# An adaLN block with attention and experts: experts three batches behind in 512-column products, queries and keys two ahead, bias added by GpSimd

## The chip, the cores and the metric

The kernel runs on one core of a Trainium2 chip. The metric is the device time of one execution in microseconds (us). Engines are named as the profile names them: PE is TensorE (PEld its weight loads), DVE VectorE, ACT ScalarE, POOL GpSimd, SP the engine that only issues DMAs.

## What is computed

16 batches of 256 tokens of 128 channels, in float32:

```python
mod = (silu(c) @ wmod).reshape(16, 6, 1, 128)            # sa, ca, ga, sb, cb, gb per batch
ga, gb = sign(ga) * max(|ga|, 0.25), the same for gb
h = layernorm(x) * (1 + ca) + sa
q, k, v = split(h @ Wqkv + bqkv)                         # 16 heads of 8 channels
Kmat = exp(-r_sigma * (|k_i|^2 + |q_j|^2 - 2 k_i . q_j))
x = x + ga * ((Kmat @ v) @ Wproj + bproj)
h = layernorm(x) * (1 + cb) + sb
mask = top 2 of softmax(h @ w_router.T + b_router)       # of 8 experts, weight 1 each
x = x + gb * sum_e mask_e * (h @ w_experts[e].T + b_experts[e])
```

## The kernel before, in words

The work is a software pipeline written out by hand: each engine has a function `step(k)` which lists its instructions for step k in order, with semaphore waits. Steps -2 and -1 are the prologue, 0 to 14 are pipelined, then come `last` (step 15) and `tail`. Step k does the attention of batch k and the other stages of batches around it. Each engine works strictly in the order of its list.

Per batch: GpSimd makes the first layernorm (`rsqrt`, `normalise`, into xn), TensorE transposes it (`turn_x`), ScalarE scales and shifts it (h1), TensorE multiplies it by the weights of queries and keys (`qk_rows`, L1001) and of the values (`values`, L1010). DVE adds the bias to queries and keys twice, into qkf and, rounded to fp32r, into hl (`queries_keys`, `high_parts`); GpSimd makes squares (sq, L411) and the low part (hl, L413); TensorE sums the squares (`norms`, L1023), ScalarE and DVE split the result (norm_hi, norm_parts, L731). SP stacks high parts, low parts and norms by DMA (`stack`) into st, of which there are two, by the parity of the batch. With that stacking one product per head gives the whole exponent.

Four score groups a step (`qk_scores(k, g)`, L962) each fill the four banks of `scores`; ScalarE takes the exponentials in two halves (L495); `pv` (L982) multiplies them by the values, in 32-column strips of the array. ScalarE copies the result out (o_sb), `project` (L1048) multiplies by wg, which GpSimd has made (`weigh`, L394, and L396, which adds the projection's bias to x); DVE adds to x (`first_residual`, L746), takes statistics (L688), GpSimd the root, DVE normalises (`normalise`, x2n), TensorE transposes (`turn_x2`, L1056), ScalarE scales (h2), DVE splits h2 in a high and a low fp32r part (`split_h2`), TensorE multiplies by the router weights (`router`, L1064). DVE's `choose` makes the mask of the two best experts: logits (L776), top 8, their indices, eq (L787), mask (L790).

The experts are four groups c of two experts each (`experts(b, c)`, L1120 to L1122). A group has, for each half of the tokens, three products of 256 columns: high by high, low by high, high by low. DVE multiplies each expert's 128 columns by its mask column and accumulates in acc (L708), 16 instructions a batch. The accumulator starts from the experts' bias: the mask is transposed (`turn_mask`), multiplied by the biases (`expert_bias`, L1084) and copied by ScalarE into acc. GpSimd's `gate` multiplies acc by the gate (L382) and adds it to x (L385).

What is done in step k before: queries and keys, norms and values of batch k+1; pv of k-1 (second half of group 2, and 3) and of k (groups 0, 1, half of 2); projection of k-1; router, mask and groups 0 and 1 of the experts of k-2, groups 2 and 3 of k-3; gate of k-3.

The ways in which products use the array matter here. Scores and the bias product have 32 or 16 rows; queries and keys, values, norms, pv, projection and router have 32 columns and lie side by side in strips; the experts' products and the transposes of xn and x2n take the full array.

## Time and profile before

| | |
|---|---|
| median of 3 runs | 221.42 us (221.41 to 222.49) |
| profiled execution | 223.4 us, of which the span from first to last instruction 221.6 |
| mean granted TensorE clock | 0.992 |
| steady step (from 60.6 us to 184.5 us of the span) | 12.06 us |
| first scores, step 0 | 14.66 us |
| first scores of step 1, 2, 3 and 15 | 25.43, 36.61, 48.57, 193.23 us |

The profile is of one execution. Busy time counts the time in which at least one instruction runs on an engine; the ends of products are modelled. In a timeline each row is a run of like instructions: its start, the time from its start to the end of the last, engine, line, operation, operands, number; idle time of the engine ahead of it stands in brackets with what released it. A product appears twice as often in it as in the program where its operands are float32 and not fp32r.

### The profile page before, as it was taken

The page shows a single profiled execution, that of the slowest core. Times are in us where ns is not written, and L with a number is a line of the kernel's source. Part 1 is how long each engine was busy: PE and PEld are TensorE (multiplying, and loading weights), DVE is VectorE, ACT ScalarE, POOL GpSimd, SP SyncE. Part 2 cuts the span into 40 slices and gives each one's busy share as a digit, 9 for nine tenths or more (in the row PEclk, how much of TensorE's full clock was granted, in tenths as well). Part 3 has the DMA queues.
Part 4 walks back from the last instruction along what each step waited for, and adds up shares of the span by engine and source line. Part 5 has one row for each costly group of instructions (what it writes and reads, how often), then busy time and mean ns, then how long its engine had stood idle before and what let it go on. Part 6 is the DMA issues. An engine that isn't in the chain of part 4 may idle for free.

```text
span 221.6 us, 8225 instructions
## 1 busy us (share of the span) xinstructions
PE 211.3 (95%) x3250; PEld 148.2 (67%) x3250; DVE 176.4 (80%) x610; ACT 163.5 (74%) x234; POOL 138.3 (62%) x204
## 2 busy tenths in 40 slices
PE   7979889899999999999999999999999999999993
PEld 6656454567676767677677767676767767666791
DVE  5876442768888898988898888889898889877884
ACT  5236888877877868698877788686879777787362
POOL 5455756564957758575849486675857594434183
PEclk9996999999999999999999999999999999999999
DMA  5565233332323332434333332324341423200001
GB/s 152 150 209 180 71 114 104 114 105 104 114 74 127 106 119 86 151 89 148 96 144 74 104 129 81 125 81 143 86 151 68 149 67 120 79 24 27 3 24 49
DMA packets 22472, 22.94 MB, mean 104 GB/s; under 512 B 2330, under 2 KB 20258, under 8 KB 22434
## 3 DMA queue, kind: packets, MB, share of 16 engines
q1 hardware_dynamic: 21962, 21.79, 30.3%
q10 hardware_dynamic: 472, 0.62, 0.9%
q8 instruction: 26, 0.43, 0.8%
q14 instruction: 12, 0.10, 0.2%
HBM read 6.65 MB, written 2.12 MB: 40 GB/s over the span
## 4 chain that ended last, share of the span: by engine, by line
PE 88%; ACT 3%; issue 2%; DVE 2%; POOL 2%; DMA 1%; POOLq 0%; DVEq 0%; ACTq 0%
PE att_ps L982 26%; PE scores L962 12%; PE qkv_ps L1001 7%; PE qkv_ps L1010 4%; PE qkv_ps L1120 3%; PE mid_ps L1048 3%; PE ffn_ps L1120 3%; PE ffn_ps L1122 3%; PE ffn_ps L1121 3%; ACT probs L495 3%; PE att_ps L1120 2%; PE scores L914 2%; PE mid_ps L1084 2%; PE qkv_ps L1122 2%; PE qkv_ps L1121 2%
## 5 line engine op out<-in xcount | busy, mean ns | idle before, releaser
L495 ACT ACTIVATE probs<-scores 128x1024 f32<-128x1024 f32 x128 | 124.3, 1022 | 12.1 <-PE scores L962 7.1
L982 PE MATMUL att_ps<-probs,vpad 128*32 128x256 f32 x1024 | 68.0, 382 | 0.0
L982 PEld LDWEIGHTS att_ps<-probs,vpad 128*32 128x32 f32 x1024 | 29.6, 109 | 17.7 <-issue 0.2
L962 PE MATMUL scores<-st 32*128 32x256 f32 x512 | 37.3, 329 | 4.2 <-ACT probs L495 2.7
L368 POOL TENSOR_TENSOR ve<-stats,eps 128x2 f32<-128x2 f32 x32 | 6.3, 195 | 44.8 <-DVE stats L688 44.8
L708 DVE SCALAR_TENSOR_TENSOR acc<-ffn_ps,mask,acc 128x128 f32<-128x128 f32 x114 | 32.0, 343 | 0.2
L962 PEld LDWEIGHTS scores<-st 32*128 32x128 f32 x512 | 23.1, 183 | 13.2 <-ACT probs L495 4.7
L411 POOL TENSOR_TENSOR sq<-qkf 128x512 f32<-128x512 f32 x15 | 15.6, 1042 | 20.8 <-DVE qkf L714 20.8
L375 POOL TENSOR_SCALAR xn<-x_all,stats,rstd 128x128 f32<-128x128 f32 x30 | 25.8, 863 | 1.6
L370 POOL TENSOR_TENSOR rstd<-ve,expo 128x2 f32<-128x2 f32 x32 | 22.8, 711 | 2.5
L708 DVE SCALAR_TENSOR_TENSOR acc<-qkv_ps,mask,acc 128x128 f32<-128x128 f32 x64 | 18.0, 344 | 7.3 <-PE qkv_ps L1122 7.3
L714 DVE TENSOR_TENSOR qkf<-qkv_ps,bqk_col 128x512 f32<-128x512 f32 x16 | 11.1, 692 | 12.1 <-PE qkv_ps L1001 12.0
L413 POOL TENSOR_TENSOR hl<-qkf,hl 128x512 fp32r<-128x512 f32 x15 | 19.4, 1292 | 0.0
L1001 PE MATMUL qkv_ps<-h,wqk_sb 128*32 128x256 f32 x256 | 17.1, 385 | 0.0
L1120 PE MATMUL ffn_ps<-we_hi,h_hi 128*128 128x256 f32 x56 | 17.1, 305 | 0.0
L502 ACT COPY acc<-mid_ps 128x256 f32<-128x256 f32 x15 | 5.6, 372 | 14.8 <-PE mid_ps L1084 14.8
L1121 PE MATMUL ffn_ps<-we_hi,h_lo 128*128 128x256 f32 x56 | 15.6, 279 | 0.0
L1122 PE MATMUL ffn_ps<-we_lo,h_hi 128*128 128x256 f32 x56 | 15.6, 279 | 0.0
L708 DVE SCALAR_TENSOR_TENSOR acc<-att_ps,mask,acc 128x128 f32<-128x128 f32 x52 | 14.6, 343 | 0.2 <-DVE acc L708 0.2
L382 POOL TENSOR_TENSOR gated<-acc,rb_all 128x256 f32<-128x256 f32 x14 | 10.3, 737 | 5.2 <-DVE acc L708 4.5
L688 DVE BATCH_NORM_STATS2 stats<-x_all 128x6 f32<-128x256 f32 x32 | 12.5, 423 | 0.1
L396 POOL TENSOR_TENSOR x_all<-x_all,rb_all 128x256 f32<-128x256 f32 x16 | 11.8, 739 | 0.0
(172 smaller groups left out, 429.6 us busy)
## 6 DMA issues: line engine op xcount, KB each, us to landing
st<-hl SPq DMA_DIRECT2D x47, 256.0 KB
rb_all<-rb_rows SPq DMA_DIRECT2D x16, 192.0 KB, 3.2
out_dram<-x_all SPq DMA_DIRECT2D x16, 128.0 KB, 1.8
x_all<-in_L_attn_x_dram SPq DMA_DIRECT2D x13, 128.0 KB, 3.0
st<-norm_parts SPq DMA_DIRECT2D x60, 16.0 KB
we_sb<-in_L_ffn_w_experts_dram SPq DMA_DIRECT2D x1, 512.0 KB, 5.4
w_mod_sb<-in_L_wmod_dram SPq DMA_DIRECT2D x1, 256.0 KB, 4.6
st<-hl ACTq DMA_DIRECT2D x1, 256.0 KB
```

The costliest lines, as they stand in the source:

```text
L370: nc.gpsimd.tensor_tensor(rstd[:, n, :], ve[:, n, :], expo[:, :], ALU.pow).then_inc(rstd_ok, 1)
L375: i = nc.gpsimd.tensor_scalar(xn[:, par, t * C:(t + 1) * C], x_all[:, b, t * C:(t + 1) * C], stats[:, 0, par, 3 * t + 1:3 * t + 2], rstd[: ...
L411: nc.gpsimd.tensor_tensor(sq[:, :, :], qkf[:, :, :], qkf[:, :, :], ALU.mult).then_inc(sq_ok, 1)
L413: nc.gpsimd.tensor_tensor(hl[:, 1:4:2, :], qkf[:, :, :], hl_f[:, 0:4:2, :], ALU.subtract).then_inc(lo_ok, 1)
L495: nc.scalar.activation(probs[:, g, 2 * half:2 * half + 2, :], scores[:, 2 * half:2 * half + 2, :], ACT.Exp, scale=two_sigma).then_inc((exp ...
L708: v.scalar_tensor_tensor(acc[:, q, t, :], y, m, acc[:, q, t, :], ALU.mult, ALU.add).then_inc(acc_step, 1)
L962: i = pe.matmul(scores[:, r, t * T:(t + 1) * T], st[rows, par, g, t * P:(t + 1) * P], st[rows, par, g, T:2 * T], start=True, stop=True)
L982: i = pe.matmul(att_ps[r * ROWS:(r + 1) * ROWS, 0:T], heads[:, g * ROWS:(g + 1) * ROWS], probs[:, g, r, t * T:(t + 1) * T], start=(g == 0 ...
L1001: i = pe.matmul(qkv_ps[m, a * T:(a + 1) * T], wqk_sb[:, a, m], h1[:, :], start=True, stop=True)
L1120: pe.matmul(dst, hi, we_hi[:, es], start=True, stop=False)
L1121: pe.matmul(dst, lo, we_hi[:, es], start=False, stop=False)
L1122: i = pe.matmul(dst, hi, we_lo[:, es], start=False, stop=True)
```

## The change

- The experts of batches 0 to 12 (`b < WIDE`, WIDE = NB - 3) are made three steps behind. A group c is now half c // 2 of the experts for half c % 2 of the tokens: three products of 512 columns. Batches 13 to 15 keep 256 columns.
- acc has two accumulators per batch for them; the first instruction into each is a multiplication, and nothing is loaded beforehand. The bias product goes, a step later, through ScalarE into bias_sb, and GpSimd's `gate`, now four steps behind, first adds the two accumulators, then bias_sb.
- Queries and keys (with high parts and low parts) are made two steps ahead, norms and values one ahead; h1 has two buffers. The first layernorm runs three ahead on GpSimd.
- The order of each engine's list is new; pv of a batch is in whole groups. The warm-up products of step 0 are gone. SP stacks a batch only when the scores of the one two before it are done.

The diff, cut to what is spoken of:

```diff
+    HE = NE // 2
+    WIDE = NB - 3
...
-        h1 = sb("h1", [P, T])
+        h1 = sb("h1", [P, 2, T])
...
-        acc = sb("acc", [P, 2, NT, C])
+        acc = sb("acc", [P, 2, 2, NT, C])
+        bias_sb = sb("bias_sb", [P, NT * C])
...
@@ stack (SP)
+                else:
+
+                    sp.wait_ge(qk_a, G * (b - 1))
+                    sp.wait_ge(qk_b, G * (b - 1))
...
@@ gate (GpSimd)
+                if b < WIDE:
+                    nc.gpsimd.tensor_tensor(wide, acc[:, par, 0, :, :], acc[:, par, 1, :, :], ALU.add).then_inc(both_ok, 1)
+                    pool.wait_ge(both_ok, b + 1)
+                    pool.wait_ge(bias_in, b + 1)
+                    nc.gpsimd.tensor_tensor(gated[:, par, :], gated[:, par, :], bias_sb[:, :], ALU.add).then_inc(bias_out, 1)
+                    pool.wait_ge(bias_out, b + 1)
...
@@ step (GpSimd), k > 0
+                if has(k - 4):
+                    gate(k - 4)
+                if has(k + 2):
+                    parts(k + 2)
+                if k > 0:
+                    weigh(k)
                 if has(k - 1):
                     rsqrt(1, k - 1, (k + 1) % 2, bn2, ve2, rstd2)
+                if k > 0 and has(k + 3):
+                    first_norm(k + 3)
...
@@ experts (VectorE)
+                if b < WIDE:
+
+                    h, t = c // NT, c % NT
+                    if c == 0 and b >= 2:
+                        dve.wait_ge(both_ok, b - 1)
+                    for e in range(HE):
+                        j = HE * c + e
+                        y = bank[:, e * C:(e + 1) * C]
+                        m = mask[:, q, t, 0, HE * h + e:HE * h + e + 1].bitcast(F32)
+                        a = acc[:, q, e % 2, t, :]
+                        if h == 0 and e < 2:
+                            v.tensor_scalar(a, y, m, None, ALU.mult).then_inc(acc_step, 1)
+                        else:
+                            dve.wait_ge(acc_step, STEPS * b + j - 1)
+                            v.scalar_tensor_tensor(a, y, m, a, ALU.mult, ALU.add).then_inc(acc_step, 1)
+                    return
...
@@ experts (TensorE)
+                if b < NB - 4 and c == 0:
+                    pe.wait_ge(norm_ok, b + 5)
+                elif b < NB - 4 and c == 1:
                     pe.wait_ge(o_ok, b + 3)
+                elif b < NB - 4 and c == 2:
+                    pe.wait_ge(m_sb, b + 1)
+                elif b < NB - 4:
+                    pe.wait_ge(acc_step, steps(b, 3 * HE))
...
-                for t in range(NT):
-                    dst = f_bank(b, c)[:, t * EC * C:(t + 1) * EC * C]
+
+                for t in (c % NT,) if b < WIDE else range(NT):
+                    dst = f_bank(b, c) if b < WIDE else f_bank(b, c)[:, t * EC * C:(t + 1) * EC * C]
...
@@ step (TensorE)
                 qk_scores(k, 0)
+                if has(k - 4):
+                    expert_bias(k - 4)
...
+                if k > 1:
+                    norms(k + 1)
                 if has(k - 1):
-                    pv(k - 1, 2, (1,))
-                if has(k - 1):
+                    pv(k - 1, 2)
                     pv(k - 1, 3)
...
+                if has(k - 3):
+                    turn_mask(k - 3)
+                qk_scores(k, 1)
...
+                if has(k - 3):
+                    experts(k - 3, 0)
+                    experts(k - 3, 1)
+                if has(k - 2):
+                    turn_x2(k - 2)
+                if k > 0 and has(k + 2):
+                    turn_x(k + 2)
+                if has(k - 3):
+                    experts(k - 3, 2)
+                qk_scores(k, 2)
...
+                if k > 0 and has(k + 2):
+                    qk_rows(k + 2)
+                pv(k, 0)
+                values(k + 1)
...
                 if has(k - 2):
                     router(k - 2)
+                qk_scores(k, 3)
+                if has(k - 1):
+                    project(k - 1)
+                pv(k, 1)
...
+                if has(k - 3):
+                    experts(k - 3, 3)
```

Three places show how the lists move. A row is a line, an operation, its output and inputs (buffer numbers left out), its shape and how many stand in a row.

On PE, in a steady step of before, from the half group of pv to the second of two expert groups that lie around the transposes (the last three rows come once more right behind):

```order
L982 MATMUL att_ps<-probs,vpad 32x256 x4
L1120 MATMUL qkv_ps<-we_hi,h_hi 128x256
L1121 MATMUL qkv_ps<-we_hi,h_lo 128x256
L1122 MATMUL qkv_ps<-we_lo,h_hi 128x256
L1120 MATMUL qkv_ps<-we_hi,h_hi 128x256
L1121 MATMUL qkv_ps<-we_hi,h_lo 128x256
L1122 MATMUL qkv_ps<-we_lo,h_hi 128x256
L1056 MATMUL mid_ps<-ident,x2n 128x128 x2
L1035 MATMUL mid_ps<-ident,xn 128x128 x2
L1120 MATMUL ffn_ps<-we_hi,h_hi 128x256
L1121 MATMUL ffn_ps<-we_hi,h_lo 128x256
L1122 MATMUL ffn_ps<-we_lo,h_hi 128x256
```

Now, from score group 1 on:

```order
L1056 MATMUL scores<-st 128x256 x8
L1253 MATMUL qkv_ps<-we_hi,h_hi 128x512
L1254 MATMUL qkv_ps<-we_hi,h_lo 128x512
L1255 MATMUL qkv_ps<-we_lo,h_hi 128x512
L1253 MATMUL att_ps<-we_hi,h_hi 128x512
L1254 MATMUL att_ps<-we_hi,h_lo 128x512
L1255 MATMUL att_ps<-we_lo,h_hi 128x512
L1165 MATMUL mid_ps<-ident,x2n 128x128 x2
L1138 MATMUL mid_ps<-ident,xn 128x128 x2
L1253 MATMUL ffn_ps<-we_hi,h_hi 128x512
L1254 MATMUL ffn_ps<-we_hi,h_lo 128x512
L1255 MATMUL ffn_ps<-we_lo,h_hi 128x512
```

Three of the four groups stand in one stretch around the transposes, with half as many products of twice the columns, and score groups on both sides of it.

On DVE, from the mask of one batch on, before (hl here and below is one tensor's name, written by two engines):

```order
L787 TENSOR_TENSOR eq<-slot_e,topi 128x32
L790 TENSOR_TENSOR mask<-eq 128x32
L708 SCALAR_TENSOR_TENSOR acc<-att_ps,mask,acc 128x128 x4
L746 TENSOR_TENSOR x_all<-mid_ps,x_all 128x256
L731 SCALAR_TENSOR_TENSOR norm_parts<-norm_hi,lo_col,qkv_ps 128x128
L688 BN_STATS stats<-x_all 128x6 x2
L762 CAST mask_t<-mid_ps 16x256
L756 TENSOR_SCALAR x2n<-x_all,stats,rstd 128x128 x2
L767 CAST h_hi<-h 128x256
L769 TENSOR_TENSOR h_lo<-h,h_hi 128x256
L738 TENSOR_TENSOR vpad<-qkv_ps,bq_all 128x32x8
L708 SCALAR_TENSOR_TENSOR acc<-ffn_ps,mask,acc 128x128 x4
```

Now:

```order
L873 TENSOR_TENSOR eq<-slot_e,topi 128x32
L876 TENSOR_TENSOR mask<-eq 128x32
L825 TENSOR_TENSOR x_all<-mid_ps,x_all 128x256
L748 BN_STATS stats<-x_all 128x6
L817 TENSOR_TENSOR vpad<-mid_ps,bq_all 128x32x8
L748 BN_STATS stats<-x_all 128x6
L768 SCALAR_TENSOR_TENSOR acc<-ffn_ps,mask,acc 128x128 x4
L851 CAST h_hi<-h 128x256
L853 TENSOR_TENSOR h_lo<-h,h_hi 128x256
L835 TENSOR_SCALAR x2n<-x_all,stats,rstd 128x128 x2
L810 SCALAR_TENSOR_TENSOR norm_parts<-norm_hi,lo_col,qkv_ps 128x128
```

The expert group moved from behind mask to behind the statistics, split_h2 (h_hi, h_lo) now stands ahead of normalise (x2n), and norm_parts, for which PE's first expert group waits, comes after all of them.

On POOL, from the first layernorm to the low parts of queries and keys, before:

```order
L375 TENSOR_SCALAR xn<-x_all,stats,rstd 128x128 x2
L382 TENSOR_TENSOR gated<-acc,rb_all 128x256
L385 TENSOR_TENSOR x_all<-x_all,gated 128x256
L394 TENSOR_TENSOR wg<-wproj_sb,rb_all 128x128
L396 TENSOR_TENSOR x_all<-x_all,rb_all 128x256
L411 TENSOR_TENSOR sq<-qkf 128x512
L413 TENSOR_TENSOR hl<-qkf,hl 128x2x256
```

Now, and on to weigh:

```order
L399 TENSOR_SCALAR xn<-x_all,stats,rstd 128x128 x2
L408 TENSOR_TENSOR gated<-acc 128x256
L411 TENSOR_TENSOR gated<-gated,bias_sb 128x256
L413 TENSOR_TENSOR gated<-gated,rb_all 128x256
L416 TENSOR_TENSOR x_all<-x_all,gated 128x256
L435 TENSOR_TENSOR sq<-qkf 128x512
L437 TENSOR_TENSOR hl<-qkf,hl 128x2x256
L425 TENSOR_TENSOR wg<-wproj_sb,rb_all 128x128
L427 TENSOR_TENSOR x_all<-x_all,rb_all 128x256
```

gate has two additions more and comes ahead of sq and hl, and weigh (wg and the addition to x) moved from ahead of sq to right behind hl.

## Rows read from the trace of the kernel before

**Rows 1.** The page, part 1: busy time by engine.

```profile
PE 211.3 (95%) x3250; PEld 148.2 (67%) x3250; DVE 176.4 (80%) x610; ACT 163.5 (74%) x234; POOL 138.3 (62%) x204
```

**Rows 2.** By stage: us; busy of PE, PEld, DVE, ACT, POOL; clock, DMA share, GB/s.

```profile
14.66:25.43 10.77, 9.87 (x124) 6.05 (x125) 6.24 (x10) 7.24 (x9) 6.36 (x7) 0.84 0.35 115
25.43:36.61 11.18, 9.48 (x157) 5.30 (x158) 3.69 (x9) 9.37 (x12) 6.96 (x12) 1.00 0.30 101
36.61:48.57 11.96, 11.18 (x189) 7.38 (x189) 7.30 (x25) 10.12 (x16) 7.61 (x11) 1.00 0.37 117
17.46:20.88 3.42, 3.42 (x24) 2.51 (x20) 2.45 (x5) 2.20 (x3) 1.82 (x2) 0.50 0.49 164
100.12:112.18 12.06, 12.06 (x205) 8.48 (x201) 10.62 (x38) 9.67 (x13) 8.38 (x13) 1.00 0.37 112
```

**Rows 3.** The timeline of PE in a steady step: start us, us, instruction.

```profile
106.83 0.38 PE L1120 MATMUL qkv_ps<-we_hi,h_hi 128*128 128x256 f32 x1
...
107.06 0.28 PE L1121 MATMUL qkv_ps<-we_hi,h_lo 128*128 128x256 f32 x1
...
107.65 0.38 PE L1056 MATMUL mid_ps<-ident,x2n 128*128 128x128 f32 x2
...
108.00 0.36 PE L1120 MATMUL ffn_ps<-we_hi,h_hi 128*128 128x256 f32 x1
...
108.88 0.50 PE L962 MATMUL scores<-st 32*128 32x256 f32 x8
...
109.32 1.07 PE L1001 MATMUL qkv_ps<-h,wqk_sb 128*32 128x256 f32 x16
...
110.20 1.48 PE L982 MATMUL att_ps<-probs,vpad 128*32 128x256 f32 x24
...
111.50 0.29 PE L1064 MATMUL mid_ps<-wr_t,h 128*32 128x8 f32 x16
```

**Rows 4.** The timeline of DVE in the same step.

```profile
100.75 0.77 DVE L787 TENSOR_TENSOR eq<-slot_e,topi 128x32 f32<-128x32 f32 x1
...
101.55 0.19 DVE L790 TENSOR_TENSOR mask<-eq 128x32 fp32r<-128x32 f32 x1
...
101.66 1.12 DVE L708 SCALAR_TENSOR_TENSOR acc<-att_ps,mask,acc 128x128 f32<-128x128 f32 x4
...
102.70 0.41 DVE L746 TENSOR_TENSOR x_all<-mid_ps,x_all 128x256 f32<-128x256 f32 x1
...
103.29 0.76 DVE L688 BATCH_NORM_STATS2 stats<-x_all 128x6 f32<-128x256 f32 x2
...
104.82 0.60 DVE L756 TENSOR_SCALAR x2n<-x_all,stats,rstd 128x128 f32<-128x128 f32 x2
...
106.33 1.12 DVE L708 SCALAR_TENSOR_TENSOR acc<-ffn_ps,mask,acc 128x128 f32<-128x128 f32 x4
...
111.91 0.17 DVE L776 TENSOR_TENSOR logit<-mid_ps,br_all 128x16 f32<-128x16 f32 x1 [0.17 <-PE mid_ps L1064]
```

**Rows 5.** The timeline of POOL in the same step.

```profile
100.17 1.30 POOL L413 TENSOR_TENSOR hl<-qkf,hl 128x512 fp32r<-128x512 f32 x1
...
103.80 0.19 POOL L368 TENSOR_TENSOR ve<-stats,eps 128x2 f32<-128x2 f32 x1 [2.33 <-DVE stats L688]
...
107.54 0.74 POOL L382 TENSOR_TENSOR gated<-acc,rb_all 128x256 f32<-128x256 f32 x1
...
109.04 0.48 POOL L394 TENSOR_TENSOR wg<-wproj_sb,rb_all 128x128 f32<-128x128 f32 x1
```

**Rows 6.** The timelines of DVE and POOL near the end.

```profile
213.50 0.41 DVE L787 TENSOR_TENSOR eq<-slot_e,topi 128x32 f32<-128x32 f32 x1
...
213.94 0.19 DVE L790 TENSOR_TENSOR mask<-eq 128x32 fp32r<-128x32 f32 x1
...
213.12 0.74 POOL L439 TENSOR_TENSOR gated<-prod 128x256 f32<-128x256 f32 x1
```

**Rows 7.** The timeline of PE, its first scores; in brackets the idle time before.

```profile
14.66 0.51 PE L962 MATMUL scores<-st 32*128 32x256 f32 x8 [1.21 <-DMA st<-norm_parts]
```

372 lines of the change are left out of this document (215 added, 157 removed).

## The prediction

> **What bounds the kernel now.** The page's first part comes first [rows 1]: PE busy 95% of the span, DVE 80%, ACT 74%, POOL 62%. A total over stages with different limits says little, so the second view is the table by stage [rows 2], one row for each of the steps 0, 1 and 2 (cut at the first product of score group 0), one for the stretch with the low clock, and one of 12.06 us that runs exactly over a steady step (from one step's experts to the next's). The reader sees two regimes. In steps 0 to 2 PE is busy 9.87 of 10.77, 9.48 of 11.18 and 11.18 of 11.96 us. In the steady step PE is busy 12.06 of 12.06 us, DVE 10.62, ACT 9.67, POOL 8.38. So PE sets the step, and DVE stands only 1.4 us below it. A change that shortens PE's step is therefore worth at most what DVE, and the loops between DVE and PE, let through.
>
> The third view is PE's timeline of a steady step [rows 3]. What counts in it is the distance between starts, because each row's own duration overlaps the next. From 107.06 to 107.65 stand five full-array products: 0.118 us each. The first of them after a section in strips takes 0.23 (106.83 to 107.06). From 106.83 to 108.88 stand twelve expert products and four transposes: 2.05 us, which I use as one piece. A score group takes 0.44 (108.88 to 109.32), queries and keys 0.88, twelve attention products 1.30 (so eight take 0.87); values has as many products of half the columns as queries and keys, 0.44.
>
> **The change, part by part.**
>
> *Experts in 512-column products.* Twelve products instead of 24 in a step. 256 columns at the granted 1.00 (2.4 GHz) are 0.107 us, and the row has 0.118; if the 0.011 stays one fixed cost of a product, 512 columns take 0.225, and 12 x 0.011 = 0.13 us of the step go. The bounds are 0.236 (nothing gained) and 0.214 (0.26 gained).
>
> *The new layout of PE's step.* Now there are three places fewer or cheaper: experts to projection is gone, norms to scores is gone, one experts to scores is new. A switch costs 0.23 - 0.118 = 0.11. Net one to two switches, 0.1 to 0.25 us; the attention products now run in longer pieces. PE alone: 12.06 - 0.13 - 0.2 = 11.7 us.
>
> *DVE.* The same work, in another order: 16 accumulate instructions (4 of them now start an accumulator rather than add to one, same shape, taken as equal). Its 10.62 us fit in 11.7, but the order makes a loop. PE's first expert product of step k now waits for norm_ok of step k's norm_rows, and DVE reaches norm_rows only after choose, first_residual, second_stats, values, first_stats, four accumulates, split_h2 and normalise; choose in turn waits for the router product, which stands on PE behind that first expert product. I close the loop with rows. DVE [rows 4]: logits to the instruction after mask, 111.91 - 12.06 = 99.85 to 101.66, 1.81 us; first_residual and norm_rows 102.70 to 103.29, 0.59; statistics now behind a wait on the residual, its 0.41 against 0.33 of distance plus some 0.05, so +0.13; two statistics 0.73 (the row's 0.76, less overlap); four accumulates 1.04; normalise, split_h2 and values 104.82 to 106.33, 1.51; the end of norm_rows beyond its distance, 0.1. Sum 5.91. PE, from first expert product to router: 2.05 + 6 more halves x 0.118 - 9 x 0.011 = 2.66, scores 0.44, queries and keys 0.88, attention 0.87, values 0.44: 5.29. Router start to logits 0.41 (111.50 to 111.91), norm_ok to PE about 0.08 (an estimate, no row has that wait). Together 11.69 us: the same as PE alone. So the step is bounded twice at 11.7.
>
> *ACT.* It has 9.67 us of work in a step, one bias copy for another. Exponentials of a group end before the next score group is asked for, in a step of 11.7 too: nothing. If that cover went, each wait would be at most one exponential, 1.02.
>
> *POOL.* Each wide batch gets two more additions of 128 x 256, at 0.74 like its other ones (the multiplication and addition of gate at 107.54 stand so): 8.38 + 1.48 = 9.9 of 11.7 us, and the step still fits. What is queued behind gate is sq and hl of the batch two ahead. sq starts 0.8 us after queries and keys reach DVE and hl ends 3.1 after that point, so 9.4 us of the step lie between hl and the next sq; weigh 1.2, the two rsqrt 2.0, xn 1.7 and gate 3.1 make 8.0 of them. Nobody waits for gate itself, as its batch is four behind.
>
> *But POOL and DVE get in each other's way.* The row for eq shows it: 0.77 us at 100.75, ending 0.05 us after POOL's hl of 100.17 + 1.30 [rows 4, 5]; later, at 213.50, it took 0.41 and ended 0.05 after POOL's 213.12 + 0.74 [rows 6]. So eq, with two inputs from SBUF, waits for the whole POOL instruction. In the step before, POOL had nothing ready after hl (next start 103.80 us, behind a wait), and mask went through in 0.19. Now weigh stands right behind hl, with proj_ps already there: wg, 0.48 [rows 5], and the x addition. Below, mask is not touched; above, it waits for the rest of wg, about 0.3 us, and both lie on the loop. The nearest row is mask at 213.94, which started 0.03 us after eq and wasn't held, but no row has POOL's next instruction already queued. I take half, 0.15: step 11.85.
> The Trainium skill (SBUF — State Buffer, "Who interferes with whom") says that whichever instruction is issued first gets the shared ports for the whole of it and the other fully blocks. By that rule eq, which waited first, passes before wg, and mask behind wg: 0.3, a step of 12.0, the second rival below. The trace agrees in eq's two durations and can't show the rest.
>
> *DMAs.* SP's stack now waits for the scores of two batches back, its queue has rows and stack interleaved, with loads first. The stack's inputs are ready most of a step before its scores start, and its seven issues take 0.6 to 0.7 us of queue each. Nothing; if the norm rows came late, high_parts on DVE would be the first to wait, and then the loop above.
>
> *Start.* Steps 0 to 2 have no experts now and lose warm-up products. Step 1 is set by ACT (9.37 us busy, plus waits for norms and heads): about 10.7 us rather than 11.18. Step 2 has lost two expert groups (1.70), a mask transpose and a bias and comes down on ACT: 10.1 us, with some waits, against 11.96. Step 0: about 10.0 for 10.77, since scores no longer queue behind warm-ups. Together -0.7 - 0.5 - 1.9 = -3.1. Step 3 lacks the bias product: -0.5.
>
> *Middle.* Ten steps (4 to 13) at 11.85 against 12.06: -2.1. Step 14 has no queries and keys (-0.88) but two bias or mask pieces more (+0.4): -0.5.
>
> *End.* The last step has four wide expert groups instead of two halves: 6 x 0.225 = 1.35, one more transposed x2 (0.2), one more bias (0.2), less what PE waited for exponentials there: +1.6. The tail after it is the same.
>
> Sum: -3.1 - 0.5 - 2.1 - 0.5 + 1.6 = -4.6 us. The profiled execution took 223.4 us with a span of 221.6; so 218.8 there, and by the same difference 216.8 against the median of 221.42.
>
> **The rivals.** (1) *Mask waits for wg each time.* Step 12.0, ten steps -0.6 instead of -2.1: -3.1 us, 218.3. For it: hl and wg back to back. Against it: mask at 213.94.
> (2) *POOL starves DVE (slower than before).* If eq, which waits on hl, loses the ports to wg and the x addition as well, choose ends 0.42 + 0.74 = 1.2 us later, in a loop without slack: step 12.9, ten steps +8.4, less 2.5 at the ends: +5.9, 227.3. It decides from 12.31 us a step on (12.06 plus a tenth of the 2.5 us won at both ends), that is from 0.6 us of delay on the loop. For it: three POOL instructions ready in a row. Against it: eq started within 0.05 us of POOL's end both times.
> (3) *The clock falls at the start.* The granted clock was 0.50 (1.2 GHz) in 17.46:20.88 [rows 2], after PE had sat idle, 1.21 us before the first scores [rows 7], and full after that stretch, which held warm-up products. They are gone; were another stretch of 3.4 us slow, a third to a half of it would be lost: +1.5, 218.3; two such, 219.8.
> (4) *The wide products don't gain and the loop is as long as PE's old step*: 12.06. Then only the ends count, -2.5: 218.9.
> (5) *512 columns at 0.214 and no hold on mask:* step 11.6, -7 us, 214.3.
>
> **How the numbers follow.** Forecast 0.42, rival 1 0.20, rival 2 0.15, rival 3 0.08, rival 4 0.07, rival 5 0.08. A measurement of this kernel can tell 0.5%, 1.1 us, from no change. The forecast's own range is 215 to 218.5; with the rivals that lie below the old time, and the edge of the one above, 213.8 to 221.8. Faster by over 0.5% takes nearly all but rival 2: 0.76; within 0.5%, pieces of 2, 3 and 4: 0.08; slower 0.16.
>
> **What would show it.** Right: steady steps of 11.7 to 11.9 us; distances of 0.225 between wide products; PE's few waits before the first expert product, released by DVE norm_parts; steps 1 and 2 near 10.5 with PE waiting for ACT. Wrong: eq or mask above 1 us with wg beside it and PE waiting for norm_ok or logits; POOL's sq late, with PE's norms behind it; a clock of 0.50 past 21 us; a last step longer by over 2.5 us.

## The result and the profile after

The changed kernel took 228.82 us (median of 4 runs, 227.90 to 229.76), the kernel before 221.95 us in runs beside it (221.41 to 224.44): a ratio of 1.0275, 95% interval 1.0223 to 1.0326. It is slower by 2.7%. Forecast were 216.8 us, 213.8 to 221.8. The profiled execution took 228.04 us with a span of 226.2, 4.6 us more than the span of 221.6 before. The ratios below leave out runs over 1.5% above the fastest of the same kernel (three of the ten of e8, one each of e12 and e13); the medians are of all runs.

The page's first part, the granted clock in 40 slices and the chain that ended last, of the changed kernel (busy times before: [rows 1]), and as a last line the same chain of the kernel before:

```profile
PE 210.2 (93%) x3084; PEld 139.1 (62%) x3084; DVE 177.9 (79%) x611; ACT 161.8 (72%) x233; POOL 157.8 (70%) x230
...
PEclk9996988999999999999999999999999999999999
...
PE 65%; DVE 19%; issue 7%; ACT 4%; POOL 2%; DMA 1%; POOLq 0%; ACTq 0%
...
PE 88%; ACT 3%; issue 2%; DVE 2%; POOL 2%; DMA 1%; POOLq 0%; DVEq 0%; ACTq 0%
```

DVE's share of the chain was 2% before and is 19% now: PE is no longer alone in what sets the end. The table by stage, cut like [rows 2] at the first product of score group 0 (steps 0 to 3, a steady step, and from the first scores of 15 to its projection):

```profile
core 0: us, PE busy (x) PEld busy (x) DVE busy (x) ACT busy (x) POOL busy (x), PEclk, DMA share, GB/s
14.28:25.91 11.63, 9.22 (x124) 4.87 (x124) 6.52 (x11) 8.17 (x10) 8.13 (x10) 0.85 0.36 121
25.91:37.81 11.90, 10.48 (x160) 5.85 (x156) 3.72 (x7) 8.23 (x12) 6.75 (x8) 0.86 0.33 103
37.81:48.33 10.52, 9.40 (x177) 5.75 (x173) 4.68 (x17) 9.16 (x13) 6.26 (x10) 1.00 0.39 115
48.33:60.50 12.17, 11.96 (x190) 7.78 (x186) 10.51 (x36) 9.84 (x13) 7.78 (x12) 1.00 0.39 119
109.30:121.48 12.18, 12.00 (x189) 7.91 (x188) 10.66 (x38) 9.56 (x13) 9.85 (x15) 1.00 0.34 110
193.96:212.06 18.10, 16.58 (x221) 10.31 (x220) 15.66 (x63) 10.62 (x16) 8.92 (x13) 1.00 0.05 16
```

| stretch (spans) | before | after | forecast | measured |
|---|---|---|---|---|
| up to first scores | 14.66 | 14.28 | 0 | -0.4 |
| steps 0 to 2 | 33.91 | 34.05 | -3.1 | +0.1 |
| step 3 | 12.06 | 12.17 | -0.5 | +0.1 |
| steps 4 to 13 | 120.75 | 121.83 | -2.1 | +1.1 |
| step 14 | 11.85 | 11.63 | -0.5 | -0.2 |
| first scores of 15 to its projection | 14.18 | 18.10 | +1.6 | +3.9 |
| the rest | 14.2 | 14.1 | 0 | 0 |

Three places, then: the steady step, the start and the end. The steady step is 12.18 us, where 11.85 was forecast. Its PE timeline, where [rows 3] has the old one:

```profile
108.40 0.50 PE L1253 MATMUL ffn_ps<-we_hi,h_hi 128*128 128x512 f32 x1
108.74 0.39 PE L1254 MATMUL ffn_ps<-we_hi,h_lo 128*128 128x512 f32 x1
108.97 0.40 PE L1255 MATMUL ffn_ps<-we_lo,h_hi 128*128 128x512 f32 x1
109.30 0.51 PE L1056 MATMUL scores<-st 32*128 32x256 f32 x8
109.98 0.41 PE L1211 MATMUL mid_ps<-be_parts,mask_t 16*128 16x128 f32 x2 [0.17 <-DVE vpad L817]
110.31 0.43 PE L1119 MATMUL qkv_ps<-sq,nw 128*32 128x128 f32 x8
110.55 1.91 PE L1076 MATMUL att_ps<-probs,vpad 128*32 128x256 f32 x32
112.39 0.29 PE L1193 MATMUL ffn_ps<-ident_r,mask 128*16 128x128 f32 x2
112.61 0.51 PE L1056 MATMUL scores<-st 32*128 32x256 f32 x8
113.05 0.51 PE L1253 MATMUL qkv_ps<-we_hi,h_hi 128*128 128x512 f32 x1
```

One wait stands in it, ahead of the bias product L1211: scores to bias are 0.68 us. DVE's timeline ahead of that, and GpSimd's beside it (before: [rows 4, 5]):

```profile
107.53 0.75 DVE L873 TENSOR_TENSOR eq<-slot_e,topi 128x32 f32<-128x32 f32 x1
108.31 0.39 DVE L876 TENSOR_TENSOR mask<-eq 128x32 fp32r<-128x32 f32 x1
108.63 0.41 DVE L825 TENSOR_TENSOR x_all<-mid_ps,x_all 128x256 f32<-128x256 f32 x1
109.08 0.43 DVE L748 BATCH_NORM_STATS2 stats<-x_all 128x6 f32<-128x256 f32 x1
109.42 0.40 DVE L817 TENSOR_TENSOR vpad<-mid_ps,bq_all 128x256 f32<-128x256 f32 x1
```

```profile
106.95 1.28 POOL L437 TENSOR_TENSOR hl<-qkf,hl 128x512 fp32r<-128x512 f32 x1
108.19 0.47 POOL L425 TENSOR_TENSOR wg<-wproj_sb,rb_all 128x128 f32<-128x128 f32 x1
```

These rows hold a loop that the prediction does not have. The bias product (k-4) writes the bank (a part of PE's output memory, here mid_ps) from which DVE unpacks the values; so it waits for `values(k)` (vpad), which ends DVE's run choose, residual, statistics, values in the step before. That run starts at the logits (106.64), which wait for the router product, and vpad ends at 109.82. The bias product stands second in PE's list, ahead of all the rest of the step, the next router product (118.42) among it. Closed with these rows, the loop is 0.41 us from router product (106.23) to logits, 3.18 to the end of vpad, 0.16 to the bias product and 8.44 to the next router product: 12.19 us, the step.

At the start the granted clock was 0.50 from 18.92 to 22.33 and from 32.57 to 35.98 us; before it was so once. At the end two waits of PE stand ahead of bias products (0.80 us, to 202.28, and 0.45 us, to 204.35); the experiments come back to both.

### The profile page after: what moved, and what is told of

Same layout as the page of the kernel before. It is cut to its first block, busy times and chain, and to the rows that moved or that the text cites. A ratio compares the mean times of both kernels' runs of the same rounds, so it can differ in the third digit from the quotient of the medians.

```text
span 226.2 us, 8009 instructions
## 1 busy us (share of the span) xinstructions
PE 210.2 (93%) x3084; PEld 139.1 (62%) x3084; DVE 177.9 (79%) x611; ACT 161.8 (72%) x233; POOL 157.8 (70%) x230
## 4 chain that ended last, share of the span: by engine, by line
PE 65%; DVE 19%; issue 7%; ACT 4%; POOL 2%; DMA 1%; POOLq 0%; ACTq 0%
PE att_ps L1076 19%; PE scores L1056 7%; PE qkv_ps L1095 6%; DVE eq L873 4%; ACT probs L539 4%; PE mid_ps L1106 3%; PE qkv_ps L1253 3%; PE qkv_ps L1119 3%; DVE vpad L817 2%; DVE x_all L825 2%; PE mid_ps L1211 2%; DVE topi L870 2%; DVE acc L768 2%; PE ffn_ps L1253 2%; PE scores L1008 2%
## 5 line engine op out<-in xcount | busy, mean ns | idle before, releaser
L1076 PEld LDWEIGHTS att_ps<-probs,vpad 128*32 128x32 f32 x1024 | 33.4, 112 | 17.1 <-issue 1.9
L1056 PEld LDWEIGHTS scores<-st 32*128 32x128 f32 x512 | 21.0, 184 | 21.3 <-issue 12.1
L768 DVE SCALAR_TENSOR_TENSOR acc<-ffn_ps,mask,acc 128x128 f32<-128x128 f32 x102 | 28.4, 340 | 0.0
L793 DVE TENSOR_TENSOR qkf<-qkv_ps,bqk_col 128x512 f32<-128x512 f32 x16 | 11.0, 690 | 10.7 <-PE qkv_ps L1095 9.5
L765 DVE TENSOR_SCALAR acc<-qkv_ps,mask 128x128 f32<-128x128 f32 x26 | 7.9, 347 | 11.7 <-PE qkv_ps L1255 11.7
L1253 PE MATMUL ffn_ps<-we_hi,h_hi 128*128 128x512 f32 (+1 forms) x30 | 14.0, 465 | 0.0
L425 POOL TENSOR_TENSOR wg<-wproj_sb,rb_all 128x128 f32<-128x128 f32 x16 | 7.4, 464 | 6.0 <-PE mid_ps L1151 5.9
L408 POOL TENSOR_TENSOR gated<-acc 128x256 f32<-128x256 f32 x13 | 9.7, 749 | 2.6 <-DVE acc L768 2.6
L1255 PE MATMUL ffn_ps<-we_lo,h_hi 128*128 128x512 f32 (+1 forms) x30 | 11.4, 380 | 0.0
L411 POOL TENSOR_TENSOR gated<-gated,bias_sb 128x256 f32<-128x256 f32 x13 | 9.6, 737 | 2.6 <-ACT bias_sb L569 1.6
L1254 PE MATMUL ffn_ps<-we_hi,h_lo 128*128 128x512 f32 (+1 forms) x30 | 11.3, 378 | 0.0
```

Of the source, the lines that this page charges most:

```text
L768: v.scalar_tensor_tensor(a, y, m, a, ALU.mult, ALU.add).then_inc(acc_step, 1)
L1056: i = pe.matmul(scores[:, r, t * T:(t + 1) * T], st[rows, par, g, t * P:(t + 1) * P], st[rows, par, g, T:2 * T], start=True, stop=True)
L1076: i = pe.matmul(att_ps[r * ROWS:(r + 1) * ROWS, 0:T], heads[:, g * ROWS:(g + 1) * ROWS], probs[:, g, r, t * T:(t + 1) * T], start=(g == 0 ...
L1253: pe.matmul(dst, hi, we_hi[:, es], start=True, stop=False)
```

## Experiments

All medians, with the ratio to the kernel before in the same runs; "step" is the steady step; "start" runs from the first scores of 0 to the first of 3; "end" from the first scores of 15 to its projection. Start, step and end are from the profiled execution. The names e1 to e16 are those of the runs.

| kernel | us | ratio, 95% | start | step | end |
|---|---|---|---|---|---|
| changed | 228.82 | 1.0275 (1.0223 to 1.0326) | 34.05 | 12.18 | 18.10 |
| bias product later (e1) | 227.36 | 1.0224 (1.0195 to 1.0253) | 34.86 | 11.96 | 18.08 |
| weigh later (e2) | 228.18 | 1.0261 (1.0239 to 1.0283) | 33.52 | 12.13 | 18.08 |
| idle products in step 1 (e3) | 227.76 | 1.0229 (1.0187 to 1.0271) | 34.78 | 12.18 | 18.09 |
| **values before statistics** (e4) | 224.53 | 1.0067 (1.0027 to 1.0107) | 34.55 | 11.76 | 18.08 |
| e4 + halves of 256 columns (e5) | 224.53 | 1.0105 (1.0047 to 1.0162) | 33.17 | 11.79 | 18.11 |
| e4 + weigh later (e11) | 229.17 | 1.0275 (1.0251 to 1.0299) | 33.81 | 12.08 | 18.04 |
| e4 + gaps filled (e6) | 225.55 | 1.0146 (1.0093 to 1.0200) | 33.68 | 11.76 | 18.10 |
| e4 + end reordered (e7) | 224.73 | 1.0110 (1.0053 to 1.0167) | 33.98 | 11.76 | 18.29 |
| e4 + gaps + end (e8) | 224.67 | 1.0055 (1.0017 to 1.0094) | 33.18 | 11.76 | 18.30 |
| e4 + GpSimd's order (e10) | 225.08 | 1.0095 (1.0061 to 1.0129) | 32.62 | 11.76 | 18.09 |
| e4 + gaps + GpSimd's order (e9) | 222.54 | 0.9971 (0.9939 to 1.0003) | 32.94 | 11.76 | 18.09 |
| e9 + end (e12) | 223.01 | 1.0014 (0.9968 to 1.0060) | 32.92 | 11.76 | 21.00 |
| e12 + thin sums (e13) | 223.19 | 0.9987 (0.9944 to 1.0030) | 33.11 | 11.76 | 18.14 |
| e9 + two stacks (e14) | 221.88 | 0.9963 (0.9930 to 0.9997) | 32.95 | 11.76 | 18.07 |
| **e14 + step 2 filled** (e16) | 221.28 | 0.9904 (0.9870 to 0.9938) | 31.29 | 11.76 | 18.10 |
| changed + gaps filled (e15) | 228.37 | 1.0257 (1.0158 to 1.0355) | 33.53 | 12.18 | 18.07 |

### The steady step

**The bias product later.** In TensorE's step, `expert_bias(k - 4)` goes behind `pv(k - 1, 2)` and `pv(k - 1, 3)`.

> Edit: on TensorE the bias product of element k-4 stands behind the two weighted sums of step k-1's element instead of right behind the first score group. Theory A (the step is bound by a loop that the prediction missed: the values' unpacking on VectorE, last thing but one of the step, ends 109.82 us in the changed kernel's trace, the bias product that waits for it stands ahead of everything of the next step on TensorE and loses 0.34 us each time, 0.68 us from score group to bias product against 0.34 us where it does not wait): the wait on the values goes, the steady step falls from 12.18 us to about 11.85 us, the ten middle steps from 121.8 to 118.5 us, and the whole from 228.8 us to about 225.5 us. Theory B (VectorE's own work, slowed by GpSimd, binds the step): the idle time appears in another place of TensorE's row, the step stays at 12.1 to 12.2 us and the whole within 0.5 us of 228.8. Theory C (the bias product was no bound and TensorE is simply busy for 12.1 us): no wait of over 0.1 us shows, no change.

No wait is left ahead of it and the step is 11.96 us, a gain of 0.22, not 0.33. The rest is the new place: from the first scores to the first expert product are 3.53 us (109.92 to 113.45), where the kernel with the bias in its old place and no wait has 3.34. The whole was expected to fall by 3.3 us and fell by some 1.1 by the ratios (0.0051 of 222), beside the longest start of all the profiles (34.86).

**The values before the statistics.** The same wait, without touching TensorE:

```diff
                 if has(k - 1):
                     first_residual(k - 1)
-                    second_stats(k - 1)
                 if k > 0:
                     values(k + 1)
+                if has(k - 1):
+                    second_stats(k - 1)
```

> Edit: VectorE unpacks the values of k+1 ahead of the second statistics of element k-1 (0.46 us or so) instead of behind them. Theory A (TensorE's bias product waits for the unpacked values): the same wait as in the first experiment shrinks without any change on TensorE; values are ready some 0.4 us earlier, the step falls by 0.3 us to about 11.85 to 11.9 us, unless the statistics that come 0.4 us later make the second normalisation late (rival B: turn_x2 then waits 0.1 to 0.4 us and the step stays at 12.1 us or more). Rival C (TensorE's own work binds): no change.

The timeline of PE in this kernel:

```profile
109.27 0.50 PE L1057 MATMUL scores<-st 32*128 32x256 f32 x8
109.61 0.33 PE L1212 MATMUL mid_ps<-be_parts,mask_t 16*128 16x128 f32 x2
109.87 0.43 PE L1120 MATMUL qkv_ps<-sq,nw 128*32 128x128 f32 x8
```

Scores to bias fell from 0.68 to 0.34 us and the step from 12.18 to 11.76, under the forecast 11.85. The ratio fell from 1.0275 to 1.0067: two lines of DVE's list are worth some 4.6 us (0.0208 of 222) of the 6.1 that the first ratio stands for. PE is now busy in all of the step (11.74 of 11.75 us). Theory A holds, rivals B and C don't.

In this kernel the loop that the prediction did close, from the router product through DVE to the norms' parts, has no slack left. DVE's norm_parts ends at 112.47 and PE's first expert product, which waits for it, starts at 112.61, 0.14 us later; where PE does wait for norm_parts (e11, below) that distance is 0.15 us. So "bounded twice at 11.7" describes this kernel, and not the changed one.

**Weigh later**, once on the changed kernel and once on the kernel with the values first: GpSimd's `weigh(k)` behind `rsqrt(1, k - 1, ...)`.

> Edit: GpSimd weighs the projection (0.47 us) behind the reciprocal root of the element before, instead of ahead of it, so that it does not stand beside VectorE's mask instruction. Theory A (the loop through VectorE's choose, residual, statistics and values to the bias product binds): mask falls from 0.38 to about 0.19 us, the values are unpacked 0.19 us earlier, the step falls by 0.15 to 0.2 us and the whole by 1.5 to 2 us, to about 227. Rival B (the later start of the weighing holds the root of the second normalisation or the projection back): the root is reached no earlier, mask falls and the time stays within 0.5 us of 228.8. Rival C (TensorE's own work binds): mask falls, the step does not.

> GpSimd weighs the projection later (as in e2_weigh_late), on top of e4_values_before_stats (224.5 us, step 11.75 us), so that VectorE's mask no longer stands beside it. Theory A (with the wait on the values gone TensorE's own work is the bound, 11.75 us): the mask instruction falls from 0.39 to 0.19 us and the step and the whole stay the same (within 0.5 us). Rival B (VectorE's chain is still in the loop): the step falls by 0.05 us or more, as it did by 0.05 us in e2_weigh_late (12.17 to 12.12).

Both expectations were wrong in the same way. Mask fell to 0.19 us in both, as it was to. But wg and the addition to x then stood beside the split of h2. PE's timeline in the first:

```profile
109.49 0.51 PE L1056 MATMUL scores<-st 32*128 32x256 f32 x8
109.99 0.41 PE L1211 MATMUL mid_ps<-be_parts,mask_t 16*128 16x128 f32 x2
...
112.63 0.51 PE L1056 MATMUL scores<-st 32*128 32x256 f32 x8
113.24 0.47 PE L1253 MATMUL qkv_ps<-we_hi,h_hi 128*128 128x512 f32 x1
```

Scores to bias fell from 0.68 to 0.50 us, by as much as mask did; scores to the first expert product rose from 0.44 to 0.61, since DVE's h_hi took 0.74 us for 0.28 and norm_parts came late. What one place won the other lost, and the step fell by 0.05 us alone. DVE's timeline in the second:

```profile
109.11 0.19 DVE L876 TENSOR_TENSOR mask<-eq 128x32 fp32r<-128x32 f32 x1
...
111.99 0.84 DVE L853 TENSOR_TENSOR h_lo<-h,h_hi 128x256 fp32r<-128x256 f32 x1
```

```profile
111.77 0.79 POOL L427 TENSOR_TENSOR x_all<-x_all,rb_all 128x256 f32<-128x256 f32 x1
```

h_lo took 0.84 for 0.42 us, the norms' parts came late and PE waited 0.25 us for them ahead of its first expert product. The step was 12.08 instead of 11.76, and the whole 4.6 us slower. A collision taken out of one place of a full loop went to a worse one. So in the changed kernel mask did wait for wg, as rival 1 said, and as it stands on the loop to the bias product, that wait was 0.2 us of the step there. With the values first it costs nothing: mask takes 0.39 us in e4 too, and PE is busy throughout.

**Halves of 256 columns**: each wide expert product as two, on top of the values first.

> Edit, on top of the values ahead of the statistics (e4_values_before_stats, 224.5 us, steady step 11.75 us): each expert product of 512 columns is two of 256, with the same banks, waits and order of groups. Theory A (the width of a product gains nothing beyond its columns: the trace shows 0.233 us for 512 columns and 0.118 us for 256): the step stays within 0.05 us of 11.75 and the whole within 0.7 us of 224.5. Rival B (the wide products save start-up, as the prediction's 0.225 us had it): twelve wide products a step would each take 0.015 us more, the step 11.93 us and the whole about 2.3 us more.

The median is the same, 224.53 us, and the step 11.79 for 11.76 (one of the ten middle steps took 12.36, with a wait of 0.57 us for the logits that no other had). In the changed kernel wide products start 0.233 us apart (108.74 to 108.97), twice the 0.118 of [rows 3]: their width gained nothing. The Trainium skill (TensorE: Matmul & The Clock Gate, Back-to-back issue gap) gives, for a product taken by itself at the full clock, 2.5 ns beside its columns, which would be 0.216 us for 512; these rows say 0.233, and they decide.

### The start

> Edit: three idle products of 128 columns on TensorE ahead of score group 2 of step 1, where the changed kernel's trace shows 0.78 us without work just before its clock goes to 0.5 for 3.4 us (32.57 to 35.99). Theory A (the second stretch at 1.2 GHz comes of these idle gaps; the gaps themselves are ScalarE's exponentials and cannot be helped): the stretch is gone, rows 32.00 to 35.92 take 1.2 to 1.7 us less, step 1 takes about 10.4 us instead of 11.9, and the whole falls by 1.2 to 1.7 us to about 227.3. Rival B (the clock falls all the same, or a little later, since a gap of 0.54 us stands behind the next two products too): no gain, up to 0.3 us lost. Rival C (the stretch goes, but the exponentials that follow bound the step anyway): step 1 falls by less than 0.5 us.

The median fell by 0.5% by the ratios, with overlapping intervals. In its profile the clock was at 0.50 from 20.00 to 30.24 us, ahead of the place that was filled; its other runs took 226.95 and 226.99 us at a granted clock of 1.0, 228.53 at 0.992. The same list of instructions in steps 0 and 1 got no stretch at half clock in one run and 10.2 us of it in another. Between these four runs the clock is worth what the expectation said of a stretch: 1.6 us from a granted clock of 1.0 to 0.992, which is one stretch of 3.4 us (the changed kernel's profile, with two, has 0.985), and 3.1 us to 0.977, which is three.

**The gaps filled**: idle products of 128 columns in the waits of steps 0 and 1, in this way:

```diff
+                        if t == 0 and r == 2 and n in (1, 2, 6):
+                            warm_up(2, P, ffn_ps if n == 6 else att_ps)
                         if t == 0 and r == 2 and n > 0:
                             pe.wait_ge(exp_b, n)
```

> Edit, on top of e4_values_before_stats: idle products of 128 columns fill TensorE's waits of steps 0 and 1 (two behind the first quarter of score groups 1 and 2 of step 0 and of group 2 of step 1, two ahead of the first norms, three ahead of the turning of element 2, three ahead of score group 2 of step 1). In e4's trace the clock stood at 0.5 from 19.63 to 29.87 us. Theory A (the half clock of the start comes of gaps in steps 0 and 1, which the changed layout has and which the layout before filled with idle products of its own): the stretch at half clock is gone or at most 3.4 us long; step 0 and step 1 together take about 20.5 us as against 22.3 us in e4 and 23.5 us in the changed kernel, and the whole is 2 to 3 us below 224.5. Rival B (the fill is not enough or not seen: the clock falls all the same, as it did in step 0 of the kernel before in spite of idle products): within 1 us of 224.5.

> The changed kernel (228.8 us, first half clock twice for 3.4 us in its trace) with the filled gaps of steps 0 and 1 alone. Theory A (GpSimd's chain binds the start): the stretches at half clock go in most runs, step 3 begins within 0.5 us of 48.3 us, and the whole stays within 0.8 us of 228.8. Rival B (the clock is worth what the slowed rows show, 1.2 to 1.7 us a stretch): 226 to 227 us.

The medians gained nothing beyond the scatter (225.55 for 224.53; 228.37 for 228.82). One reason is that the fill did not hold the clock: it was 1.0 in one of four runs (e6, 224.21 us; the others 225.23 to 225.95) and in two of four (e15, 226.91 and 227.67; the others 229.07 and 229.99 at 0.992 and 0.993). Another shows in the profiles, which both have 1.0 up to the end and starts of 33.68 and 33.53 us all the same. PE's timeline of step 2 in the changed kernel with the gaps filled:

```profile
40.29 0.44 PE L1167 MATMUL mid_ps<-ident,x2n 128*128 128x128 f32 x2
42.20 0.44 PE L1140 MATMUL mid_ps<-ident,xn 128*128 128x128 f32 x2 [1.48 <-POOL xn L399]
...
47.08 0.65 PE L1153 MATMUL mid_ps<-wg,o_sb 128*32 128x128 f32 x16 [0.87 <-DVE logit L860]
```

and GpSimd's beside it:

```profile
36.20 1.27 POOL L437 TENSOR_TENSOR hl<-qkf,hl 128x512 fp32r<-128x512 f32 x1 [0.75 <-DVE hl L799]
37.43 0.46 POOL L425 TENSOR_TENSOR wg<-wproj_sb,rb_all 128x128 f32<-128x128 f32 x1
37.85 0.73 POOL L427 TENSOR_TENSOR x_all<-x_all,rb_all 128x256 f32<-128x256 f32 x1
...
40.56 1.58 POOL L399 TENSOR_SCALAR xn<-x_all,stats,rstd 128x128 f32<-128x128 f32 x2
```

xn of 4 ends at 42.14 us here and at 41.89 in the changed kernel with its two slow stretches; counted from the first scores (14.98 and 14.28) that is 0.45 us sooner, and no more. GpSimd's chain has its own pace, and most of what PE wins ahead of it, it waits for.

**GpSimd's order.** Squares of 2 ahead of the normalising of 3; the first normalisation of 4 at the end of step 0 (its statistics too, on DVE).

```diff
                     weigh(0)
-                    first_norm(3)
+                    rsqrt(0, 3, 1, bn1, ve1, rstd1)
+                    squares(2)
+                    normalise(3, 1)
+                    low_parts(2)
+                    first_norm(4)
```

> Edit, on top of the values ahead of the statistics and of the filled gaps (e6_fill_gaps, 225.6 us): GpSimd's order in steps 0 and 1. The squares of element 2 stand ahead of the normalising of 3, and the whole first normalisation of element 4 is made at the end of step 0, with its statistics on VectorE, instead of at the end of step 1 behind the low parts of 3. In the trace of e8 the turning of element 4 waited 1.51 us for it, the norms of 2 waited 0.90 us for the squares, and its step 3 began at 48.12 us where the changed kernel's began at 48.33 in spite of the clock. Theory A (the start is bound by GpSimd's chain, so what full clock gives in steps 0 and 1 is given back in step 2): both waits go, step 3 begins 1.5 to 2.4 us earlier and the whole is 223.2 to 224 us. Rival B (the six transfers of an element's stack, issued one behind the other, bind the start): the turning no longer waits, but the high parts of 3 or the scores do, and the gain is under 0.5 us.

> The same GpSimd order on e4_values_before_stats alone (224.5 us), without the idle products. Theory A (GpSimd binds the start, and the clock does not matter much): 1 to 2 us less than 224.5, as with the fill. Rival B (with GpSimd's waits gone the half clock is what binds): under 0.5 us less, and the fill of e9 is needed for the gain. Rival C (the transfers bind): neither gains.

With the gaps filled 222.54 us, 1.7% less than with the fill alone by the ratios; without, 225.08, no gain. Its runs say which of the two is missing: 223.00 at a granted clock of 0.999, 224.54 to 225.69 at 0.977 and 0.985. So by the medians order and fill each gave nothing alone, and together some 2 us. Part of it is how often the clock stays up: at 0.999 or more in 8 of 10 runs with both, in one of four with either alone. The one such run with the fill alone took 224.21 us, the eight with both 222.3 us in the mean, so the order seems to gain at full clock too; one run is little to go by. In the profile of the first PE still waits 0.85 us in step 2, for x2n, and DVE's row says for what:

```profile
35.15 0.69 DVE L809 TENSOR_TENSOR hl<-qkv_ps,bqk_col 128x512 fp32r<-128x512 f32 x1 [2.08 <-DMA st<-norm_parts]
```

**Two stacks.** hl gets a second buffer, by the parity of the element, so that high parts wait for the transfers of two elements back.

> On top of e9_gpsimd_start (222.5 us): the buffer of high and low parts of queries and keys is doubled, so VectorE's high parts of an element no longer wait until the six transfers of the element before have landed (in e9 GpSimd's low parts of 3 began 1.72 us late for that, and the turning of x2 of 1 waited 0.85 us in step 2). Theory A (the transfers bind the start once GpSimd's order is mended): that wait goes, step 3 begins 0.6 to 0.9 us earlier, steady steps are unchanged at 11.76 us, the whole is 0.5 to 0.9 us below e9. Rival B (another wait takes its place: the transfers themselves, or the exponentials, 0.2 to 0.5 us ahead of most score groups): under 0.3 us.

The wait is gone. The median is 221.88, 0.66 us less than without, but in other runs, and the intervals of the ratios overlap; the runs at a granted clock of 0.999 or more have means of 221.6 and 222.3 us. In its profile step 2 now waits for exponentials, and the clock stood at 0.50 from 42.32 to 45.73: a gain at half clock again. So those waits were filled as well:

> On top of e14_two_stacks (221.9 us): idle products also in step 2, two ahead of its third score group and two behind that group's first quarter. In e14's trace TensorE waited twice 0.53 us there for exponentials, and its clock stood at 0.5 from 42.32 to 45.73 us: rows 41.97 to 45.85 took 1.6 us more than in e15 at full clock. e14's runs of granted clock 1.0 had a mean of 221.6 us, those of 0.992 one of 222.9. Theory A (with GpSimd's order and the transfers mended, TensorE's clock is what bounds the start, so it now counts): the clock stays at 1.0 in nearly all runs, step 3 begins at about 46.4 us instead of 48.0, and the median is 220.8 to 221.6 us, 0.4 to 0.8% under the kernel before. Rival B (the clock falls later instead, in step 3 or 4, or another chain takes over): 221.7 to 222.3 us, as e14.

The start is 31.29 us, the granted clock 0.999 or 1.0 in all 11 runs, the median 221.28 us, a ratio of 0.9904 (0.9870 to 0.9938): 1.0% under the kernel before and 3.6% under the changed one by the ratios. Some of that is the other kernel's clock; its runs at 0.999 or more in this batch took 222.07 to 223.17, and 221.28 is 0.8% less than their median (222.97).

### The end

> Edit, on top of e4_values_before_stats, in the last part alone: VectorE does the first residual and second statistics of element 14 ahead of the third expert group of 12; TensorE puts the bias product of 12 behind the first weighted sum of 15 and the first expert group of 13 ahead of its own bias product. Theory A (the waits of 0.80 and 0.45 us ahead of the two bias products are order, not work): first scores of 15 to its projection take 17.0 us or so instead of 18.1, the whole 0.8 to 1.2 us less than 224.5. Rival B (VectorE's queue is full there, so the wait moves to the turning of x2 of 14 or to the next expert group): under 0.4 us less.

> Both edits above together with e4_values_before_stats. If they are independent, the gains add: 224.5 less 2 to 3 less 0.8 to 1.2, so 220.5 to 221.5 us, at or just under the kernel before (222.5 in these runs). If the start's gain is taken away again by the clock, about 223.5.

> GpSimd's order at the start and the filled gaps (e9_gpsimd_start, 222.5 us) together with the reordered end of e7_end, which alone gained nothing. Theory A (VectorE's queue binds the end, whatever the order on TensorE): first scores of 15 to its projection stay at 18.0 to 18.4 us (18.10 in the changed kernel, 18.29 in e7) and the whole within 0.5 us of e9. Rival B (the end's order was masked by the scatter of the start in e7): up to 0.8 us less.

DVE's first residual and statistics of 14 went ahead of the third expert group of 12, and on TensorE `pv(b, 0)` ahead of `expert_bias(b - 3)` and `experts(b - 2, 0)` ahead of `expert_bias(b - 2)`. The end gained nothing in any of the three (18.29, 18.30 and 21.00 us for 18.1). The ratio of the second is 0.9% under that of the filled gaps alone, but not for its end; its profile reaches step 3 0.5 us sooner, and the sum of gains that was expected (220.5 to 221.5 us) did not come. 0.80 + 0.45 us of waits became these, in the profile of the first:

```profile
199.88 0.28 PE L1194 MATMUL mid_ps<-ident_r,mask 128*16 128x128 f32 x2 [0.67 <-DVE bias_sb L846]
200.45 0.38 PE L1254 MATMUL qkv_ps<-we_hi,h_hi 128*128 128x256 f32 x1 [0.29 <-DVE h_lo L853]
...
202.41 0.44 PE L1166 MATMUL mid_ps<-ident,x2n 128*128 128x128 f32 x2 [0.64 <-DVE x2n L835]
```

The third has the same three waits, and in its profile the clock was at 0.50 from 200.5 to 207.3 us, after the first two of them; that is the 2.9 us of its end. Seven of its ten runs had a granted clock of 0.992 or less, and two of ten without the new end (e9). Only this one profile shows where the clock fell, so that the new order is the reason is likely and not shown.

Is it DVE's work, then? A probe takes some from it and none from PE; it leaves out part of the output (for element 12, 112 of 128 columns of the last two groups' sums):

```diff
+                        w = 16 if b == NB - 4 and c >= 2 else C
-                        y = bank[:, e * C:(e + 1) * C]
+                        y = bank[:, e * C:e * C + w]
...
-                        a = acc[:, q, e % 2, t, :]
+                        a = acc[:, q, e % 2, t, 0:w]
```

> A probe, on top of e12_start_and_end: for element 12 alone, the weighted sums of its last two groups of four products are made over 16 of 128 columns each, so this part of the output is left out; number and order of all instructions stay. It takes some 1.0 to 1.3 us from VectorE's queue in the end and nothing from TensorE. Theory A (VectorE's queue binds the end: the expert sums of 12, which the layout's third step of delay has moved there, stand ahead of the residual, the split and the normalising of 14): first scores of 15 to its projection fall from 18.1 to 18.3 us to 17.0 to 17.3 us, and the whole by 0.9 to 1.2 us against e12. Rival B (TensorE's added work, four wide groups and one bias product, is the whole of the end's loss): no change.

The sums of four took 0.64 us for 1.11, so DVE had some 0.9 us less to do, and the end is 18.14 us, at a granted clock of 1.0, for the 18.29 of e7. Theory A falls. The waits only change their releasers:

```profile
198.30 0.28 PE L1210 MATMUL mid_ps<-ident_r,mask 128*16 128x128 f32 x2 [0.61 <-DVE bias_sb L857]
198.86 0.39 PE L1270 MATMUL qkv_ps<-we_hi,h_hi 128*128 128x256 f32 x1 [0.29 <-DVE h_lo L864]
...
200.76 0.41 PE L1182 MATMUL mid_ps<-ident,x2n 128*128 128x128 f32 x2 [0.55 <-ACT acc L556]
```

The first and the third are handovers of one bank, mid_ps: bias product of 12, its copy, mask of 13, its copy, bias product of 13, its copy, x2n of 14, all in turn. That the bank is what holds the end by 1.5 us was not tried with another bank and stays an argument. The larger part of the 3.9 us is work that moved there: PE is busy 16.58 of the 18.10 us, which is 2.4 more than the whole of that stretch before.

## Why the prediction was wrong

- **"PE alone: 11.7 us"** was right: 11.76 us when nothing holds it.
- **"12 x 0.011 = 0.13 us of the step go"** was wrong: a product's excess over its columns grew with it (0.118 us for 256, 0.233 for 512), so 12 wide products save 0.04 us. The step without waits is 0.30 us shorter than the old one; what gave that, if not the width, must be the switches, which were taken at 0.2 (argued, not tried).
- **"I close the loop with rows"** is the step that failed. I closed one loop, from the router to the norms' parts, found 11.69 us and took it for the only one. It had slack in the trace (norms' parts end 112.62, the expert product starts 113.05, so 0.43 us, and 0.15 is the distance where PE waits). Its size was about right, as e4 shows; its term of 0.08 us from norm_ok to PE measured 0.15 in e11. The bias product's four waits (`expert_bias`: m_sb, logit_ok, x1_ok, v_ok) stood in the kernel, among them the one on the values, and I priced the wait of the moved bias product at nothing. Taking that wait away gave 0.42 us a step, more than the 0.33 by which the forecast was off. Rival 2's 227.3 us is near the measured 228.82 by chance: its mechanism did not occur.
- **Mask and wg.** Of the price, "about 0.3 us" or nothing, with half taken (0.15), the 0.39 us of mask for 0.19 shows 0.2. The rule of the Trainium skill (SBUF — State Buffer, Who interferes with whom) that the first issued has the shared ports for the whole instruction fits these rows: eq, waiting since hl, went ahead of wg; mask, behind it, waited. The price by that rule, "a step of 12.0", is that of rival 1, not of "the second rival below". Rival 2, that eq too would lose to wg, didn't come: eq took 0.75 us. That mask lies "on the loop" is true of both loops; the 0.2 us cost a step through the one to the bias product, which the prediction did not have.
- **Start, step 2 "comes down on ACT: 10.1 us".** It took 10.52, with PE waiting for exponentials as forecast (1.03 us); steps 0 and 1 took 11.63 and 11.90 for 10.0 and 10.7, with a slow stretch in each. At full clock (e15) the three took 10.60, 11.10 and 11.83, the last with the waits for GpSimd and DVE shown above. I summed each engine's load and did not follow an element through it: GpSimd's list (low parts, weigh, two roots, xn), the one hl buffer and its six transfers are a chain with no slack while the pipeline fills. Priced by removing them, order, buffer and clock together are 2.8 us of the 3.2 missing (34.05 to 31.29, with the values first in the latter as well).
- **Rival 3, the clock, "+1.5"** had the right mechanism and size for a stretch, at a chance of 0.08 much too small. Two stretches came, both lasting past 21 us, as the sign of being wrong had it. Their share of the 6.9 us was not isolated: runs of one kernel differ by 1.6 (e3) and 2.2 us (e15) between no such stretch and one, but the starts of the profiles at full clock are only 0.5 us shorter (34.05 to 33.53).
- **End, "+1.6"** counted products and no handovers: +2.4 of work and 1.5 of waits. It took in two wide groups more, and nothing for the whole groups of pv and both bias products' turns on mid_ps.
- **The chances.** A loop's closing figure 0.01 us off PE's own figure, with the loops through the other waits unread, does not bear 0.76 for faster.

## What to carry to other kernels

When a product moves, list every semaphore that it waits on, and close a loop through each; the one that binds may belong to the cheapest instruction (here a bias product of 0.33 us), and then two lines of another engine's order are worth as much as the whole redesign was forecast to gain (4.6 us here). In a fill phase follow one element through all engines and buffers; a mended clock, order or buffer may show little in a median until the others are mended too, so try them together before giving one up, and sort the runs by their granted clock before reading a median. On an engine that is 90% busy, moving an instruction out of one collision is worth a look at what it will stand beside next.
